# Two gated layers with routed experts: SyncE's DMAs at both joins in other places, a second PSUM bank for four shared experts, and waits in place of the barrier behind the experts

## Chip, core and metric

The program runs on one core of a Trainium2 chip. The metric is the device time of one execution in microseconds (us), given as the median of several executions.

## What is computed

`x` has 64 blocks of 128 tokens with 256 features. Four steps follow each other, each with a gate and a residual:

```python
x = x + tanh(g_xattn[0]) * attention0(layernorm(x), ctx)      # 16 heads, softmax over 128 keys
x = x + tanh(g_ffn[0])   * experts(layernorm(x))              # 64 experts, 8 a token, at most 256 tokens each
x = x + tanh(g_xattn[1]) * attention1(layernorm(x), ctx, mask)
x = x + tanh(g_ffn[1])   * quantised_ffn(layernorm(x))        # needs a maximum over all tokens
# inside experts:
shared = silu(x @ shared_gate.T) * (x @ shared_up.T) @ shared_down.T      # for every token
return routed + shared
```

## The kernel before

**Stages.** The program has one instruction stream per engine, written out by hand, and semaphores between them. Its order: attention 0 with routing (64 blocks, in slots that each hold pieces of up to ten blocks), the experts, attention 1, and two passes of the quantised feed-forward. SyncE (`sp`) issues almost all DMAs, strictly in program order; a wait on it holds up everything behind. `phase_end` (line 270) is a barrier: an engine drains, adds 1 to `phase_done` and waits for a count. Barrier 2 (all five engines) stands between attention 0 and the experts, barrier 3 (TensorE, ScalarE, VectorE) between the experts and attention 1.

**Attention 0** (`attention_sp`, `attention_pe`, ...). In slot s, `stage(lag)` is block s - lag. Per slot SyncE loads a block's context and x, stores the block for the experts to accumulate on (`store`), its normalised tokens transposed (`store_transposed`, into `tokens_t`), its row with gate weights (`store_row`) and its routing counts (`store_steps`, read back by `load_steps`). Some slots near the end carry extra loads: `ffn_weights_in` (the feed-forward's weights, and the first four context pairs, `load_pair`), `first_expert_weights`, `attention_weights(sp, 1, ...)` and `load_shared`.

**Experts** (`expert_slots`). Slot s has, on TensorE: `slot_steps`, `rows_t` (transposes of gathered rows), `keys_or_values`, `up`, `shared_down`, `down`, `shared_up`. Routed expert s, s-1 and s-2 are at different steps of it. GpSimd gathers an expert's 256 rows (2 indirect DMAs) and adds its results (2 more). Two other strands of 64 pieces each are spread over the slots by tables: `PAIR_AT` places the keys and values of attention 1 (`keys_or_values` on TensorE, `copy_pair` on ScalarE, `keep_pair` on SyncE), and `SHARED_AT` the shared expert of 128 tokens (`shared_up`, `shared_tanh`, `shared_silu`, `shared_down`, `shared_out`, `keep_shared`). Slots that a table leaves out have no such piece. The first pieces run in attention 0's last slots and ahead of barrier 2, the last ones behind the last routed expert (slots E+1 to E+4, E = 64).

**Banks.** A shared expert's products stay in one PSUM bank from `shared_up` until `shared_out` has read it. Pieces 0 and 1 have banks 7 and 4, all later ones bank 7, so that

```python
            if n < SHARED_EARLY:
                pe.wait_ge(sem("at_out"), NB)
                pe.wait_ge(sem("qm_done"), NB)
            else:
                wait(pe, "sh_out", n)
```

makes the next `shared_up` wait for ScalarE's `shared_out` of the piece before it. Bank 4 is `down`'s bank from expert 0 on, and attention 1's.

**The second join.** `first_sums` (slot `SUMS_AT` = E + 5 on SyncE) waits for all additions of the experts, then loads for blocks 0 and 1 both halves of the routed sum and the shared part. GpSimd adds the halves (`experts_sum`), VectorE adds the row and makes the statistics (`first_sum`, `first_stats`), GpSimd raises to -1/2, ScalarE normalises (`normalise_first`), TensorE transposes (`transposes`). In attention 1 SyncE's slot loads keys and values (`load_keys_values`) and sums (`load_sums`) of later blocks.

## Time and profile before

| | us |
|---|---|
| median of three runs | 1859.84 (1858.9 to 1864.16) |
| the profiled execution, its own time | 1864.53 |
| its span | 1862.8 |
| TensorE busy / weight loads | 1724.2 / 1349.8 |
| VectorE busy | 1386.4 |
| ScalarE busy | 1180.8 |
| GpSimd busy | 612.5 |

Times in the profile are counted from the span's start. Attention 0 fills the stretch to about 638, the experts that from about 652 to 1137, attention 1 begins at 1156. PE is TensorE, DVE VectorE, ACT ScalarE, POOL GpSimd, SPq SyncE's issuing of DMAs. The granted clock is a share of TensorE's full speed.

### The profile page before, as it was taken

The page shows a single profiled execution, that of the slowest core. Times are in us where ns is not written, and L with a number is a line of the kernel's source. Part 1 is how long each engine was busy: PE and PEld are TensorE (multiplying, and loading weights), DVE is VectorE, ACT ScalarE, POOL GpSimd, SP SyncE. Part 2 cuts the span into 40 slices and gives each one's busy share as a digit, 9 for nine tenths or more (in the row PEclk, how much of TensorE's full clock was granted, in tenths as well). Part 3 has the DMA queues.
Part 4 walks back from the last instruction along what each step waited for, and adds up shares of the span by engine and source line. Part 5 has one row for each costly group of instructions (what it writes and reads, how often), then busy time and mean ns, then how long its engine had stood idle before and what let it go on. Part 6 is the DMA issues. An engine that isn't in the chain of part 4 may idle for free.

```text
span 1862.8 us, 54548 instructions
## 1 busy us (share of the span) xinstructions
PE 1724.2 (93%) x20198; PEld 1349.8 (72%) x20208; DVE 1386.4 (74%) x4589; ACT 1180.8 (63%) x2411; POOL 612.5 (33%) x617
## 2 busy tenths in 40 slices
PE   5999999999999799999999998899999999968855
PEld 4788888888887578888888887677777777733334
DVE  4788888888888637655454544788888888759988
ACT  2777777777777423333333333788888888858875
POOL 1000000000000037777777774222223222211147
PEclk8999999999999999999999999999999999989989
DMA  3233333333324558989898886233323322213265
GB/s 97 69 94 94 97 97 97 103 98 98 94 94 146 171 163 208 233 210 229 214 220 215 219 196 142 87 93 94 89 87 91 97 88 87 59 57 136 102 268 184
DMA packets 231350, 247.65 MB, mean 133 GB/s; under 512 B 29680, under 2 KB 207216, under 8 KB 228912
## 3 DMA queue, kind: packets, MB, share of 16 engines
q1 hardware_dynamic: 206272, 205.54, 34.4%
q0 software_dynamic: 24816, 38.62, 11.5%
q8 instruction: 164, 2.69, 0.6%
q14 instruction: 98, 0.80, 0.2%
HBM read 142.40 MB, written 101.66 MB: 131 GB/s over the span
## 4 chain that ended last, share of the span: by engine, by line
PE 63%; DVE 24%; ACT 8%; issue 2%; DMA 1%; SPq 1%; POOLq 0%; POOL 0%; DVEq 0%; ACTq 0%
DVE mt L928 15%; PE tiles L454 8%; PE tiles L437 8%; PE bank L519 6%; ACT pt L689 6%; PE bank L398 6%; PE tiles L1437 6%; PE bank L382 6%; PE bank L482 3%; PE tiles L421 3%; PE bank L549 3%; PE bank L1449 3%; PE bank L408 3%; DVE hmax L1824 3%; PE tiles L1419 2%
## 5 line engine op out<-in xcount | busy, mean ns | idle before, releaser
L2084 POOL TENSOR_TENSOR rstd<-var,minus_half 128x2 f32<-128x2 f32 x140 | 97.9, 699 | 728.7 <-DVE var L1007 710.0
L928 DVE TENSOR_REDUCE mt<-tiles 128x16 f32<-128x2048 f32 x128 | 293.5, 2293 | 58.8 <-PE tiles L437 58.8
L689 ACT ACTIVATE pt<-tiles 128x2048 f32<-128x2048 f32 x128 | 240.7, 1881 | 48.7 <-PE tiles L454 48.7
L1610 POOL DMA_INDIRECT accumulator<-ye,tid x128 | 208.4, 1628 | 87.6 <-DVE ye L1554 59.0
L1554 DVE TENSOR_SCALAR ye<-bank,xr 128x256 f32<-128x256 f32 x128 | 56.0, 479 | 157.5 <-PE bank L1449 157.5
L1595 POOL DMA_INDIRECT xr<-token_rows,tid x128 | 137.4, 1074 | 78.8 <-DVE tid L1530 41.2
L519 PE MATMUL bank<-xt,w_q 128*128 128x128 f32 x1024 | 156.3, 287 | 0.9 <-ACT xt L697 0.9
L454 PE MATMUL tiles<-qm,qkp 32*128 32x128 f32 x4096 | 151.1, 284 | 6.2 <-DVE mt L928 2.3
L437 PE MATMUL tiles<-qkp 32*128 32x256 f32 x2048 | 150.6, 407 | 3.3 <-ACT qkp L711 3.3
L454 PEld LDWEIGHTS tiles<-qm,qkp 32*128 32x128 f32 x4096 | 126.6, 187 | 35.8 <-DVE mt L928 21.1
L519 PEld LDWEIGHTS bank<-xt,w_q 128*128 128x128 f32 x1024 | 133.1, 196 | 14.7 <-issue 12.9
L482 PE MATMUL bank<-pt,vx 128*32 128x128 f32 x4096 | 139.2, 277 | 2.7 <-ACT pt L689 1.7
L482 PEld LDWEIGHTS bank<-pt,vx 128*32 128x32 f32 x4096 | 104.6, 110 | 45.3 <-issue 40.8
L549 PE MATMUL bank<-w_o,at 128*128 128x256 f32 x512 | 131.8, 380 | 0.5 <-ACT at L778 0.5
L437 PEld LDWEIGHTS tiles<-qkp 32*128 32x128 f32 x2048 | 87.3, 185 | 42.7 <-issue 27.1
L665 ACT ACTIVATE res<-bank 128x256 f32<-128x256 f32 x64 | 24.6, 385 | 143.7 <-PE bank L398 139.3
L940 DVE SCALAR_TENSOR_TENSOR qm<-bank,keep,qkp 128x256 f32<-128x256 f32 x256 | 110.1, 472 | 6.6 <-PE bank L468 6.3
L2107 POOL TENSOR_TENSOR res<-res,bias 128x256 f32<-128x256 f32 x64 | 46.8, 731 | 200.7 <-ACT xn L746 200.7
L709 ACT ACTIVATE qkp<-bank,qb 128x128 f32<-128x128 f32 x256 | 88.8, 372 | 34.3 <-PE bank L519 34.2
L711 ACT ACTIVATE qkp<-bank,kb,keep 128x128 f32<-128x128 f32 x256 | 106.2, 483 | 0.0
L724 ACT ACTIVATE qkp<-cxax,kb,keep 128x128 f32<-128x128 f32 x256 | 105.4, 485 | 0.0
L549 PEld LDWEIGHTS bank<-w_o,at 128*128 128x128 f32 x512 | 87.3, 190 | 8.0 <-ACT at L778 0.7
(252 smaller groups left out, 4098.2 us busy)
## 6 DMA issues: line engine op xcount, KB each, us to landing
keys_values<-res SPq DMA_DIRECT2D x64, 256.0 KB, 3.0
cxax<-keys_values SPq DMA_DIRECT2D x128, 128.0 KB, 2.5
cxax<-accumulator SPq DMA_DIRECT2D x128, 128.0 KB, 2.3
hidden_away<-h_ring SPq DMA_DIRECT2D x8, 1536.0 KB, 5.1
token_rows<-pay SPq DMA_DIRECT2D x64, 160.0 KB, 1.8
pt<-in_expert_up SPq DMA_DIRECT2D x36, 256.0 KB, 3.5
cxax<-in_ctx SPq DMA_DIRECT2D x64, 128.0 KB, 2.2
res<-in_x SPq DMA_DIRECT2D x64, 128.0 KB, 2.3
```

The source lines that it names most:

```text
L382: last = nc.tensor.matmul(kv_bank(n)[:, k * D:(k + 1) * D], weights_, moving, start=(c == 0), stop=(c == KC - 1))
L398: last = nc.tensor.matmul(shared_bank(n)[:, m * FS + j * P:m * FS + (j + 1) * P], w[:, c, j * P:(j + 1) * P], sxt[n % SHARED_IN][:, c, :], ...
L437: last = nc.tensor.matmul(both, qt[r % 2][rows, j, :], kp[r][rows, :, j, :], start=(L == 0), stop=True, skip_group_check=(L == 1))
L454: last = nc.tensor.matmul(tiles[:, i, n * P:(n + 1) * P], kp[r][rows, e, j, :], qm[rows, e, j, :], start=(L == 0), stop=True, skip_group_c ...
L482: last = nc.tensor.matmul(bank[7][32 * h:32 * h + 32, g * P:(g + 1) * P], vx[r][:, GH * g + h, :], pt[p][:, i, n * P:(n + 1) * P], start=T ...
L519: last = nc.tensor.matmul(o_, w[:, c, j * P:(j + 1) * P], (cx[r] if n else xt[p])[:, c, :], start=(c == 0), stop=(c == KC - 1))
L549: last = nc.tensor.matmul(bank[6][:, 0:D], at[r % 2][:, c, :], w_o[:, c, :], start=(L == 1 and c == 0), stop=(c == KC - 1))
L689: nc.scalar.activation(pt[r % 2][:, :, :], tiles[:, :, :], ACT.Exp).then_inc(sem("exp_done"), 1)
L928: nc.vector.tensor_reduce(mt[:, :].rearrange("p (i n c) -> p i n c", i=RT, n=2 * KC)[:, :, :, 0], tiles[:, :, :].rearrange("p i (n k) -> p ...
L1437: last = nc.tensor.matmul(bank[2 + p][:, n * CAP:(n + 1) * CAP], w[k][:, c, :], xrt[p][:, c, :], start=(c == 0), stop=(c == KC - 1))
L1595: nc.gpsimd.indirect_dma_start(out=xr[n % ROWS_IN][:, h, :], out_offset=None, in_=rows[:, :], in_offset=bass.IndirectOffsetOnAxis(ap=tid[n ...
L1610: nc.gpsimd.indirect_dma_start(out=acc[p][:, :], out_offset=bass.IndirectOffsetOnAxis(ap=tid[b % 8][:, h:h + 1], axis=0), in_=ye[r][:, h, ...
```

## The change

- SyncE in attention 0: `ffn_weights_in` comes behind the slot's stores, and no longer loads the first context pairs; these come in the two next slots, also behind the stores. `load_shared` comes a slot earlier. Of the weights of experts 1 to 6, those of 1 to 3 stay in their place, 4 and 5 go behind the last stores and 6 behind `keep_pair`; the last `load_steps` goes ahead of `keep_pair`. Layer 1's `attention_weights` go into expert slot 6 (`ATTENTION_IN_AT`), on the same semaphore as the key and value weights.
- Shared experts 3 and 62 get bank 4 (1 had it); a `shared_up` next to one of these waits only for the output two before it. Expert 0's `down` waits for shared output 3, and shared expert 62 for the last reading of bank 4.
- `PAIR_AT` leaves out 13 slots instead of 11, and its last two pieces run in new slots E+5 and E+6; `keep_pair` of these two is issued in attention 1's slots (`LATE_KEPT`). `SHARED_AT` leaves out slot 57 instead of 54.
- `first_sums` comes in slot E+4.
- Barrier 3 is gone. ScalarE's first normalisation waits for the last `down`, and TensorE's first transpose for all shared outputs and all copies of keys and values.

```diff
-        PHASES = {1: 5, 2: 10, 3: 13, 4: 18, 5: 23}
+        PHASES = {1: 5, 2: 10, 4: 15, 5: 20}
...
-            for s in range(-MAP_AHEAD, E + 6):
+            for s in range(-MAP_AHEAD, E + 7):
...
-        PAIR_AT = numbered([-7, -6, -5, -4, -3, -2, -1] + [s for s in range(E) if s not in (5, 9, 14, 21, 27, 33, 39, 45, 51, 57, 62)]
-                           + [E + 1, E + 2, E + 3, E + 4])
-        SHARED_AT = numbered([-5, -4, -3, -2, -1] + [s for s in range(E) if s not in (8, 20, 23, 30, 36, 42, 48, 54)]
+        SHARED_IN_FOUR = (1, 3, NB - 2)
+        LATE_KEPT = {2: E - 2, 3: E - 1}
+        PAIR_AT = numbered([-7, -6, -5, -4, -3, -2, -1] + [s for s in range(E) if s not in (5, 9, 14, 19, 24, 29, 34, 39, 44, 49, 54, 59, 62)]
+                           + [E + 1, E + 2, E + 3, E + 4, E + 5, E + 6])
+        SHARED_AT = numbered([-5, -4, -3, -2, -1] + [s for s in range(E) if s not in (8, 20, 23, 30, 36, 42, 48, 57)]
...
-            return bank[4] if n < SHARED_EARLY and n % 2 else bank[7]
+            return bank[4] if n in SHARED_IN_FOUR else bank[7]
...
+            elif n in SHARED_IN_FOUR or n - 1 in SHARED_IN_FOUR:
+                pe.wait_ge(sem("sh_out"), n - 1)
             else:
-                wait(pe, "sh_out", n)
+                pe.wait_ge(sem("sh_out"), n)
+            if n == NB - 2:
+                pe.wait_ge(sem("e_y_done"), E)
...
+                    if b == 0:
+                        pe.wait_ge(sem("sh_out"), NB)
+                        pe.wait_ge(sem("kv_out"), E)
...
+                if L == 1 and b == 0:
+                    act.wait_ge(sem("e_down_done"), E)
...
-        FIRST_SUMS, SUMS_AT = 2, E + 5
+        FIRST_SUMS, SUMS_AT = 2, E + 4
...
                         load_sums(sp, stage(-3))
+                        if stage(-3)[0] in LATE_KEPT:
+                            n = LATE_KEPT[stage(-3)[0]]
+                            keep_pair(sp, (n, n))
...
-                    if stage(4) is not None and stage(4)[0] == NB - 1:
-                        sp.wait_ge(sem("o_done_0"), NB)
-                        attention_weights(sp, 1, "w_in")
-                    if stage(5) is not None and stage(5)[0] == NB - 1:
-                        for n in range(SHARED_IN):
-                            load_shared(sp, (n, n))
-                    if stage(5) is not None and stage(5)[0] == ROOM_TO:
-                        ffn_weights_in(sp)
                     load_steps(stage(7))
                     store_steps(stage(6))
                     store(stage(4))
+                    if stage(4) is not None and stage(4)[0] == NB - 1:
+                        for n in range(SHARED_IN):
+                            load_shared(sp, (n, n))
                     store_transposed(stage(5))
+                    if stage(5) is not None and stage(5)[0] == ROOM_TO:
+                        ffn_weights_in(sp)
+                    if stage(5) is not None and ROOM_TO < stage(5)[0] <= ROOM_TO + 2:
+                        for j in range(2):
+                            load_pair(sp, 2 * (stage(5)[0] - ROOM_TO - 1) + j)
...
-                        first_expert_weights(sp, EARLY_FREE, WEIGHT_BUFFERS)
+                        first_expert_weights(sp, EARLY_FREE, 4)
...
             if L == 0:
+                first_expert_weights(sp, 4, 6)
+                load_steps((NB - 1, (NB - 1) % 4))
                 for n in range(KV_EARLY - 1):
                     keep_pair(sp, (n, n))
-                load_steps((NB - 1, (NB - 1) % 4))
+                first_expert_weights(sp, 6, WEIGHT_BUFFERS)
...
-                keep_pair(sp, PAIR_AT.get(s - 1))
+                if s <= E + 5:
+                    keep_pair(sp, PAIR_AT.get(s - 1))
                 keep_shared(sp, SHARED_AT.get(s - 2))
+                if stage(0) is not None and stage(0)[0] == ATTENTION_IN_AT:
+                    attention_weights(sp, 1, "w_in")
...
+                if b == 0:
+                    pe.wait_ge(sem("sh_out"), 4)
```

The other edits drop the three `phase_end(..., 3)`, renumber the waits on `w_in`, and take `load_pair` out of `ffn_weights_in`.

**SyncE, last blocks of attention 0, before.** The names are destination and source; `res` with `tokens_t` is `load_shared`, `table_rows` with `steps_out` is `store_steps`.

```order
L1956 DMA w_o<-in_L_xattn_wo 128x2x256
L1958 DMA bias_col<-in_L_xattn_bq 128x2
L1958 DMA bias_col<-in_L_xattn_bk 128x2
L1958 DMA bias_col<-in_L_xattn_bv 128x2
L1959 DMA bias<-in_L_xattn_bo 128x256
L1298 DMA table<-table_rows 2x4160
L1289 DMA table_rows<-steps_out 64x130
L1266 DMA accumulator<-res 128x256
L1267 DMA accumulator<-zt 128x256
L1274 DMA tokens_t<-x2t 128x256
L1281 DMA token_rows<-pay 128x320
L1200 DMA res<-tokens_t 128x256 x3
```

The same place in the changed kernel (its own line numbers):

```order
L1292 DMA token_rows<-pay 128x320
L1309 DMA table<-table_rows 2x4160
L1300 DMA table_rows<-steps_out 64x130
L1277 DMA accumulator<-res 128x256
L1278 DMA accumulator<-zt 128x256
L1211 DMA res<-tokens_t 128x256 x3
L1285 DMA tokens_t<-x2t 128x256
L1292 DMA token_rows<-pay 128x320
```

The six attention weights are gone from here, and the three loads of tokens stand ahead of the last two stores of this slot.

**SyncE, its last DMAs ahead of barrier 2, before:**

```order
L1298 DMA table<-table_rows 2x4160
L1289 DMA table_rows<-steps_out 64x130
L1281 DMA token_rows<-pay 128x320
L1189 DMA keys_values<-res 128x512 x2
L1662 DMA res<-in_ctx 128x2x128 x2
L1189 DMA keys_values<-res 128x512
L1298 DMA table<-table_rows 2x4160
```

and in the changed kernel:

```order
L1309 DMA table<-table_rows 2x4160
L1300 DMA table_rows<-steps_out 64x130
L1292 DMA token_rows<-pay 128x320
L1370 DMA pt<-in_expert_up 128x512
L1371 DMA on<-in_L_ffn_w 128x256
L1370 DMA qm<-in_expert_up 128x512
L1371 DMA xt<-in_L_ffn_w 128x256
L1309 DMA table<-table_rows 2x4160
L1200 DMA keys_values<-res 128x512 x2
L1681 DMA res<-in_ctx 128x2x128 x2
L1200 DMA keys_values<-res 128x512
L1370 DMA cxax<-in_expert_up 128x512
```

The last reading of the table now has four loads of weights ahead of it, and the stores of keys and values behind it.

**TensorE, end of the experts, before.** `w_k` and `w_v` are pieces of `keys_or_values`, `w_sg` and `w_su` a `shared_up`, `w_sd` a `shared_down`, `ident,xn` attention 1's first transpose.

```order
L382 MATMUL bank<-res,w_k 128x256 x4
L408 MATMUL bank<-w_sd,res 128x256 x2
L398 MATMUL bank<-res,w_sg 128x128 x4
L398 MATMUL bank<-res,w_su 128x128 x4
L382 MATMUL bank<-w_v,res 128x256 x4
L408 MATMUL bank<-w_sd,res 128x256 x2
L499 MATMUL bank<-ident,xn 128x128 x2
```

and in the changed kernel:

```order
L384 MATMUL bank<-res,w_k 128x256 x4
L414 MATMUL bank<-w_sd,res 128x256 x2
L404 MATMUL bank<-res,w_sg 128x128 x4
L404 MATMUL bank<-res,w_su 128x128 x4
L384 MATMUL bank<-w_v,res 128x256 x4
L414 MATMUL bank<-w_sd,res 128x256 x2
L384 MATMUL bank<-res,w_k 128x256 x4
L384 MATMUL bank<-w_v,res 128x256 x4
L508 MATMUL bank<-ident,xn 128x128 x2
```

Two pieces of keys and values now stand behind the last shared expert.

## Rows read from the trace of the kernel before

**Rows 1.** The page, the chain that ended last: share by engine.
```profile
PE 63%; DVE 24%; ACT 8%; issue 2%; DMA 1%; SPq 1%; POOLq 0%; POOL 0%; DVEq 0%; ACTq 0%
```
**Rows 2.** Windows: start:end, length, busy us (xcount) of the engines, clock, DMA share, GB/s.
```profile
750.00:850.00 100.00, 100.00 (x600) 87.55 (x599) 59.85 (x214) 33.97 (x68) 76.09 (x55) 1.00 0.89 224
1050.00:1136.00 86.00, 85.90 (x506) 75.56 (x505) 40.63 (x141) 26.15 (x55) 59.12 (x44) 1.00 0.79 186
1155.00:1160.00 5.00, 3.37 (x28) 2.42 (x28) 3.81 (x10) 3.60 (x10) 3.12 (x5) 0.50 0.40 111
1175.00:1180.00 5.00, 5.00 (x70) 3.47 (x70) 3.40 (x5) 1.37 (x5) 1.19 (x2) 0.63 0.01 3
```
**Rows 3.** Chain in order of time, first join: start us, us, what.
```profile
639.69 2.42 DMA tokens_t<-x2t
...
646.40 2.14 DMA keys_values<-res
649.04 2.71 DMA table<-table_rows
651.88 0.23 PE bank L1392
```
**Rows 4.** Timeline, SyncE's queue, end of attention 0.
```profile
582.95 5.86 SPq L1662 DMA_DIRECT2D res<-in_ctx  x8
...
630.14 0.43 SPq L1354 DMA_DIRECT2D pt<-in_expert_up  x1
...
634.41 0.43 SPq L1956 DMA_DIRECT2D w_q<-in_L_xattn_wq  x1
...
640.76 1.43 SPq L1200 DMA_DIRECT2D res<-tokens_t  x3
```
**Rows 5.** Timeline, VectorE and ScalarE, end of attention 0.
```profile
589.13 2.29 DVE L928 TENSOR_REDUCE mt<-tiles 128x16 f32<-128x2048 f32 x1 [0.39 <-PE tiles L437]
600.04 2.29 DVE L928 TENSOR_REDUCE mt<-tiles 128x16 f32<-128x2048 f32 x1 [1.53 <-PE tiles L437]
...
595.14 0.37 ACT L788 COPY x2t<-bank 128x256 f32<-128x256 f32 x1 [1.71 <-DMA tokens_t<-x2t]
640.95 0.27 ACT L798 CAST steps_out<-bank 64x129 bf16<-64x129 f32 x1 [4.19 <-DMA table_rows<-steps_out]
649.71 0.19 ACT L2122 ACTIVATE sig<-clips 128x2 f32<-128x2 f32 x1
```
**Rows 6.** Timeline, TensorE, first join.
```profile
638.20 0.22 PE L608 MATMUL bank<-fall,sel 128*64 128x129 bf16 x1
643.14 2.07 PE L398 MATMUL bank<-res,w_sg 128*128 128x128 f32 x8 [4.71 <-DMA res<-tokens_t]
652.99 3.68 PE L382 MATMUL bank<-res,w_k 128*128 128x256 f32 x8
658.19 1.13 PE L398 MATMUL bank<-res,w_sg 128*128 128x128 f32 x8 [0.66 <-ACT res L675]
```
**Rows 7.** Timeline, TensorE, second join.
```profile
1136.66 1.05 PE L398 MATMUL bank<-res,w_sg 128*128 128x128 f32 x8
1138.44 1.89 PE L382 MATMUL bank<-w_v,res 128*128 128x256 f32 x8
1140.17 1.03 PE L408 MATMUL bank<-w_sd,res 128*128 128x256 f32 x4
1156.17 0.66 PE L499 MATMUL bank<-ident,xn 128*128 128x128 f32 x2 [4.43 <-ACT xn L746]
```
**Rows 8.** Timelines of ScalarE and GpSimd, second join.
```profile
1150.92 0.59 ACT L657 COPY res<-bank 128x512 f32<-128x512 f32 x1 [1.34 <-PE bank L382]
1155.47 0.60 ACT L746 ACTIVATE xn<-res,nmr,rstd 128x256 f32<-128x256 f32 x1 [3.22 <-DVE nmr L1011]
1141.14 1.56 POOL L1610 DMA_INDIRECT accumulator<-ye,tid x1 [0.30 <-issue]
```

**Rows 9.** Chain in order of time, second join.
```profile
1148.37 3.28 DMA res<-shared_out
```

More of the change, by code:

```diff
@@ L370, in keys_or_values @@
             if n == 0:
-                pe.wait_ge(sem("wkv_in"), 16 * 2)
+                pe.wait_ge(sem("w_in"), 16 * 10)
                 pe.wait_ge(sem("exp_done"), NB)
@@ L1562, in next_layer @@
                 elif e[0] == E // 4 + 4:
-                    dve.wait_ge(sem("w_in"), 16 * 14)
+                    dve.wait_ge(sem("w_in"), 16 * 16)
                     scale_queries(dve, 1)
@@ L1650, in ffn_weights_in @@
             sp.dma_start(wdraw[:, :, :], a["L1_ffn_w_down"].rearrange("(k p) i -> p k i", p=P)).then_inc(sem("ffn_w_in2"), 16)
-            for j in range(4):
-                load_pair(sp, j)
         def ffn_weights_out(sp, n):
@@ L1702, in flamingo_gated_two_layers @@
         MASKS_IN_AT = {2: 0, 4: 1}
+        ATTENTION_IN_AT = 6
         def ffn_chunks(body, nb, more):
@@ L1962, in keys_values_weights @@
             for dst, src in ((w_k, "L1_xattn_wk"), (w_v, "L1_xattn_wv")):
-                sp.dma_start(dst[:, :, :], a[src].rearrange("(k p) n -> p k n", p=P)).then_inc(sem("wkv_in"), 16)
+                sp.dma_start(dst[:, :, :], a[src].rearrange("(k p) n -> p k n", p=P)).then_inc(sem("w_in"), 16)
         def scale_queries(dve, L):
@@ L2124, in _ @@
             experts_act(act)
-            phase_end(act, 3)
             attention_act(act, 1)
@@ L2142, in _ @@
             experts_pe(pe)
-            phase_end(pe, 3)
             attention_pe(pe, 1)
@@ L2196, in _ @@
             experts_dve(dve)
-            phase_end(dve, 3)
             attention_dve(dve, 1)
```

## Prediction

> **What bounds the kernel now.** I read the chain that ended last, then the windows, then the timelines of each engine at the two joins. The chain lies 63% on TensorE and 24% on VectorE [rows 1]. In the experts TensorE alone bounds: it is busy 100.00 of 100 us and 85.90 of 86 at the stage's end, at full clock [rows 2]. So a piece of TensorE work that leaves this stage shortens it by its whole length, and a delay of the stage's start moves everything behind it. The edits lie where this does not hold, at the joins.
>
> At the first join the chain leaves the compute engines: a store of tokens, loads of them, stores of keys and values, the last load of the table, barrier, TensorE [rows 3]. SyncE's queue makes it late. From 626 to 634 it issues weights of six experts, from 634.41 six loads for attention 1, and only at 640.76 the three loads of tokens [rows 4]. TensorE ends routing at 638.42 and waits 4.71 us for them [rows 6]. ScalarE's last piece ahead of the barrier ends at 649.90 [rows 5], but SyncE holds the barrier until the table of 649.04 has landed, 2.71 us later; TensorE goes on at 651.88 [rows 3].
>
> At the second join the sums are requested from 1147.5 on, the last load of a block takes 3.28 us to land [rows 9], and GpSimd, VectorE and ScalarE follow before TensorE's first transpose at 1156.17, after 4.43 us of idle time [rows 7].
>
> **The change, part by part.** Everything is counted in the profiled execution, whose own time is 1864.53.
>
> *Feed-forward weights behind the stores.* SyncE's burst has eight context loads alone for 5.86 us [rows 4], with five loads of weights ahead of them and the slot's stores behind. ScalarE then waits 1.71 us for a store of tokens, and VectorE's maxima are 10.91 us apart (589.13 to 600.04) [rows 5]; one slot takes 9.15 us by its neighbours, 10.91 less the 1.76 that this stall makes of it. With the stores first and the contexts in two later slots the stall goes: **1.8 us**. Bounds: 0, where the landing and not the issue is late, and 1.8.
>
> *First join.* The third of the early experts' weights starts at 630.14 and its pair of issues ends at 631.05. An issue takes 0.48 us (three in 1.43) [rows 4]. Five others (row, table, counts, block, zeros) bring SyncE to 633.6, where it now issues the tokens; landing as before (640.76 to 643.14, 2.4 us) they are there at 636, ahead of TensorE's 638.42. So the shared experts start 4.7 us earlier, and their strand, 6.8 us long (643.14 to 649.90) [rows 5, 6], ends at 645.2 or, at full clock, 644.2. ScalarE's wait of 4.19 us for a store of counts [rows 5] goes too, since ten issues ahead of that store are gone. SyncE: the last counts are on it at 638.9; store, row (0.6) and four weights (1.9) end at 641.7; the table's load needs 2.7 to land, 644.4. Behind it stand two stores of keys and values, two contexts, a third store that waits 2.1 us for the first one [rows 3], and two weights: SyncE ends at 645.9. The barrier opens there, TensorE starts at 646.1 instead of 651.88: **5.8 us**. Bounds: 7.2, where only the other engines' 644.2 to 645.2 count and I have put two issues too many, and 3, if the landings in this crowded stretch take twice as long. I take the middle way since each step is a row.
>
> *Two banks.* Behind the barrier TensorE waits 0.66 us ahead of each `shared_up` for ScalarE's `shared_out` [rows 6], five times until expert 0's `down` fills the gap. Pieces 2, 3 and 4 lose the wait, 5 and 6 keep it, as bank 4 is taken: 3 x 0.66 = **2.0 us**. Hidden below it is only ScalarE and VectorE's part of a piece, covered by the 1.7 us of keys and values. Bounds 0.7 and 2.0.
>
> *Two pairs fewer in the experts.* A piece of keys and values is 1.73 us of TensorE (1138.44 to 1140.17) [rows 7]. Two leave: **3.5 us**, all of it while TensorE bounds. GpSimd is the cover: it is busy 76.09 us of 100 with 55 pieces [rows 2], and about 0.3 us stands between them [rows 8], so 92 of 100. The stage is 485 us for 68 slots (651.88 to 1136.66), 7.1 each, and GpSimd needs 0.92 of that, 6.5; 3.5 us less leave it room. Bounds 0 and 3.5.
>
> *Second join.* Measured from the last routed expert (1136.66), TensorE has 15.1 us of work and waits (1156.17 less 4.43 is 1151.74) [rows 7]. It gains two pieces (+3.5), loses two waits of 0.66 (-1.3), and the last piece waits for ScalarE's copy of the one before, in the same bank (+0.8, from the 0.59 of a copy) [rows 8]: 18.1. ScalarE must copy it (0.59) and normalise (0.60) [rows 8], so the first transpose comes at 19.4; it came at 19.5. The sums are ready earlier: GpSimd's last addition starts at 1141.14 [rows 8] and lands some 4 us later, 8.5 after the mark, where the loads came at 10.8; their chain of 8.7 us ends at 17.2. So the sums stop being late and TensorE's own strand, with ScalarE behind, is what comes last: **0.1 us**, bounds -1 and 2. The barrier itself is free either way: its three engines are done at about 1152, with TensorE's strand, and the data are not.
>
> *Waits added.* ScalarE's for the last `down` and TensorE's for all outputs hold nothing, since both engines come there later by program order. SyncE's store of pair 62 now stands ahead of block 3's sums and waits for a copy 16 us behind the mark; block 3 is needed some 8 us later. Six loads more in slot 6 cost SyncE 3 us of a 7.1 us slot in which it has half free. Nothing.
>
> *Clock.* TensorE's granted clock fell after idle stretches: eight products of keys and values took 3.68 us behind the first barrier [rows 6] against 1.89 at full clock [rows 7], and the granted clock was 0.50 in 1155 to 1160 [rows 2], the lower of its two levels, behind the idle 4.43. At the second join idle time shrinks to some 1.3 us in one piece. Full clock would give back half of 3.37 us of busy time, 1.7; I take **1.0** for both joins, with 0 and 5.3 as ends (1.7, 1.8 behind the barrier, and 0.37 x 5.0 in 1175 to 1180 [rows 2]).
>
> The Trainium skill ("TensorE: Matmul & The Clock Gate", "What's actually happening") says that the throttled level is the default and activity releases it. By that rule both joins, emptier before, would run warmer now, and the sum would be some 3 us more; the trace agrees as far as the fall behind idle goes, but it also shows a fall at 1175 with TensorE at work.
>
> Sum: 1.8 + 5.8 + 2.0 + 3.5 + 0.1 + 1.0 = 14.2. The profiled execution would take 1850.3. The median of the runs shown is 4.7 lower than that execution, so I forecast **1845.6 us**.
>
> **Rivals.**
> 1. *The clock stays up at both joins.* For: less idle time at both. Against: some 3 us of idle time are left ahead of the first barrier (643 to 646), and the fall at 1175. It gives 5.3 where I took 1.0: 1841.3. Chance 0.13.
> 2. *GpSimd becomes the bound of the experts.* Slots without a pair take TensorE some 5.4 us (7.1 less 1.7), an expert takes GpSimd 6.5, and there are 13 instead of 11 of them. Then the 3.5 us come back as waits for rows: 1849.1. Against: TensorE never waited with 11. Chance 0.12.
> 3. *The DMA engines, not SyncE's order, made the stores and tokens late.* Then the first term goes and half of the second: 1845.6 + 1.8 + 2.9 = 1850.3. Against: TensorE's wait of 4.71 ends 2.4 us after the issue, a usual landing. Chance 0.08. The Trainium skill ("DMA: Bandwidth & Descriptors", "Rules for kernel authors") holds that all issuing engines feed the same 16 DMA engines; if their backlog decides, another place in the queue buys nothing, which is this rival.
> 4. *The order was covered anyway*, and what is won at the joins is waited for later (attention 1 at the same time as before): about 1860. Chance 0.03.
> 5. *Slower: gathered rows come late.* DMA engines are at 0.89 in the experts [rows 2]. Denser TensorE work and six more loads could push the gathers beyond their lead, so that TensorE waits for each expert's rows. It decides from (14.2 + 5.6) / 64 = 0.31 us per expert; at 0.5 it gives 1845.6 + 32 = 1878. Against: not one wait for rows now. Chance 0.02.
>
> **The numbers.** My forecast has the rest, 0.62, and alone reaches from 1842 to 1850. The range takes in rivals 1 and most of 2 and 3: 1839 to 1852. A measurement can tell 0.3%, 5.6 us, from no change, so faster means below 1854.3: cases 1 to 3 and the forecast make 0.95, less 0.02 for several terms at their low ends: 0.93. Within 0.3%: 0.05. Slower: 0.02.
>
> **What would show it.** Maxima of VectorE 9.15 apart throughout the last full slots; TensorE's first shared expert right behind the last counts, without a wait for tokens; its first piece behind the barrier 7 to 8 us earlier than 651.88; no wait ahead of the shared experts 2 to 4; last routed expert 13 us earlier than 1136.66; first transpose 19 to 20 us behind it, and released by ScalarE's copy, not by the sums. Wrong would be a wait of TensorE in the experts, a barrier still held past 648 by a landing, or a first transpose over 21 us behind the last expert.

## The result, and the profile after

| | before | changed |
|---|---|---|
| median, us | 1860.47 (1856.15 to 1864.74, 12 executions) | 1850.94 (1843.01 to 1855.44, 12 executions) |
| ratio to before | | 0.9949, 95% interval 0.9936 to 0.9962 |
| the profiled execution: own time / span | 1864.53 / 1862.8 | 1851.82 / 1850.1 |

The change makes the kernel 9.5 us faster in the medians; 14.2 were forecast. The profiled executions differ by 12.7, but not all of that is the change's: VectorE's maximum at 570.82 before stands at 568.32 after, in a stretch that nothing of the change touches. So spans can't be compared to the microsecond here, and I compare stretches between marks that both traces have. The mark "last `down`" is the first product behind it (1136.66 before, 1123.33 after), as in the prediction.

| stretch, us | before | after | gain | forecast |
|---|---|---|---|---|
| start to the maximum at 570.82 / 568.32 | 570.82 | 568.32 | 2.50 | not the change's |
| from there to the last counts (PE `fall,sel`) | 67.38 | 65.60 | 1.78 | 1.8 |
| last counts to TensorE's first piece behind the barrier | 13.68 | 9.89 | 3.79 | 5.8 |
| from there to expert 0's `down` | 38.54 | 36.74 | 1.80 | 2.0 |
| expert 0's `down` to the last `down` | 446.24 | 442.79 | 3.45 | 3.5 |
| last `down` to the first transpose of attention 1 | 19.51 | 19.06 | 0.45 | 0.1 |
| first transpose to ScalarE's second exponential | 24.86 | 26.09 | -1.23 | 1.0, clock, both joins |
| second exponential to the end | 681.8 | 681.6 | 0.2 | 0 |

The stretches that the change touches give 10.0 (1.78 + 3.79 + 1.80 + 3.45 + 0.45 - 1.23), near the 9.5 of the medians.

One execution of all the runs below, of e7_fill_first, took 1993.12 us at a mean granted clock of 0.84 and is left out of the medians and ratios.

The page of after, share of the chain by engine, against [rows 1]: the shape of the kernel is the same.

```profile
PE 64%; DVE 24%; ACT 8%; issue 2%; SPq 1%; DMA 1%; POOLq 0%; POOL 0%; DVEq 0%; ACTq 0%
```

Windows of after: the experts ([rows 2] before), then the first join and the ramp of attention 1.

```profile
640.00:645.00 5.00, 0.51 (x3) 0.23 (x3) 0.48 (x2) 0.00 (x0) 0.00 (x0) 0.82 0.89 292
645.00:650.00 5.00, 5.00 (x13) 3.98 (x13) 1.27 (x8) 0.58 (x1) 2.18 (x2) 0.50 0.74 226
750.00:850.00 100.00, 100.00 (x607) 87.78 (x607) 59.45 (x217) 33.33 (x67) 75.77 (x56) 1.00 0.89 220
...
1147.00:1152.00 5.00, 4.06 (x26) 2.88 (x23) 3.76 (x5) 2.80 (x9) 1.30 (x2) 0.50 0.46 133
1152.00:1157.00 5.00, 5.00 (x42) 3.54 (x43) 3.38 (x6) 2.00 (x5) 2.12 (x3) 0.50 0.43 131
```

TensorE still fills the experts entirely (100.00 of 100), with GpSimd at 75.77, so two pieces fewer count in full. But directly behind the first barrier, and for ten microseconds of the ramp (the first slots of attention 1, until its engines follow each other without gaps), the granted clock is 0.50, the lower of its two levels.

**End of attention 0.** Timelines of VectorE and ScalarE, against [rows 5]:

```profile
586.61 2.29 DVE L939 TENSOR_REDUCE mt<-tiles 128x16 f32<-128x2048 f32 x1 [0.38 <-PE tiles L443]
595.76 2.29 DVE L939 TENSOR_REDUCE mt<-tiles 128x16 f32<-128x2048 f32 x1 [0.45 <-PE tiles L443]
...
590.87 0.37 ACT L799 COPY x2t<-bank 128x256 f32<-128x256 f32 x1
```

The maxima are 9.15 apart where one gap was 10.91, and ScalarE's copy no longer waits for a store of tokens.

**First join.** SyncE's queue of after; the mark is the last counts at 633.92:

```profile
634.56 0.48 SPq L1309 DMA_DIRECT2D table<-table_rows  x1
635.09 0.48 SPq L1300 DMA_DIRECT2D table_rows<-steps_out  x1
635.61 0.58 SPq L1292 DMA_DIRECT2D token_rows<-pay  x1
636.23 0.43 SPq L1370 DMA_DIRECT2D pt<-in_expert_up  x1
...
638.21 0.48 SPq L1309 DMA_DIRECT2D table<-table_rows  x1
638.74 0.87 SPq L1200 DMA_DIRECT2D keys_values<-res  x2
639.66 1.25 SPq L1681 DMA_DIRECT2D res<-in_ctx  x2
642.06 0.34 SPq L1200 DMA_DIRECT2D keys_values<-res  x1
642.44 0.44 SPq L1370 DMA_DIRECT2D cxax<-in_expert_up  x1
642.92 0.45 SPq L1371 DMA_DIRECT2D xt<-in_L_ffn_w  x1
```

The chain of after over the same stretch, in order of time, against [rows 3]:

```profile
632.41 2.14 DMA table_rows<-steps_out
...
638.74 3.25 DMA keys_values<-res
...
642.06 0.34 SPq L1200
```

The third store of keys and values waits for the first one to land, 3.25 us after that one's issue (2.14 before [rows 3]); for 1.1 of them SyncE is idle, and the weights of expert 6 stand behind it. SyncE reaches the barrier at 643.4. TensorE, against [rows 6]:

```profile
633.92 0.22 PE L617 MATMUL bank<-fall,sel 128*64 128x129 bf16 x1
...
643.81 0.22 PE L1411 MATMUL bank<-table,halves_tri 128*128 128x32 bf16 x1 [5.04 <-SPq L272]
644.71 0.40 PE L1423 MATMUL bank<-table,begun 64*128 64x130 bf16 x2 [0.68 <-DVE begun L1532]
645.03 3.78 PE L384 MATMUL bank<-res,w_k 128*128 128x256 f32 x8
648.61 1.75 PE L414 MATMUL bank<-w_sd,res 128*128 128x256 f32 x4
650.19 1.05 PE L404 MATMUL bank<-res,w_sg 128*128 128x128 f32 x8
...
665.77 1.13 PE L404 MATMUL bank<-res,w_sg 128*128 128x128 f32 x8 [0.66 <-ACT res L684]
```

The wait of 4.71 us for tokens is gone, and 5.04 us of waiting for SyncE at the barrier has come in its place. The first eight products of keys and values behind it take 3.78 us, as they took 3.68 before. The wait of 0.66 us for ScalarE is left only from the fifth piece on.

**Second join.** TensorE of after, against [rows 7], and ScalarE, against [rows 8]:

```profile
1139.26 1.97 PE L384 MATMUL bank<-w_v,res 128*128 128x256 f32 x8 [0.77 <-ACT res L666]
1142.40 0.44 PE L508 MATMUL bank<-ident,xn 128*128 128x128 f32 x2 [1.17 <-ACT xn L757]
```

```profile
1141.26 0.58 ACT L666 COPY res<-bank 128x512 f32<-128x512 f32 x1 [2.15 <-PE bank L384]
1141.74 0.60 ACT L757 ACTIVATE xn<-res,nmr,rstd 128x256 f32<-128x256 f32 x1
```

The first transpose comes behind ScalarE's normalisation, which comes behind its copy of the last piece. The sums are no longer late: VectorE has the statistics' last value at 1138.28 + 0.69, 2.8 us before ScalarE uses it:

```profile
1138.28 0.69 DVE L1022 SCALAR_TENSOR_TENSOR nmr<-mv,rstd 128x2 f32<-128x2 f32 x1 [0.83 <-POOL rstd L2104]
```

### The profile page after: what moved, and what is told of

Its sections match the earlier page's. It is cut to its first block, busy times and chain, and to the rows that moved or that the text cites. A ratio compares the mean times of both kernels' runs of the same rounds, so it can differ in the third digit from the quotient of the medians.

```text
span 1850.1 us, 54546 instructions
## 1 busy us (share of the span) xinstructions
PE 1720.9 (93%) x20198; PEld 1348.2 (73%) x20208; DVE 1385.3 (75%) x4589; ACT 1179.3 (64%) x2411; POOL 611.1 (33%) x617
## 4 chain that ended last, share of the span: by engine, by line
PE 64%; DVE 24%; ACT 8%; issue 2%; SPq 1%; DMA 1%; POOLq 0%; POOL 0%; DVEq 0%; ACTq 0%
DVE mt L939 15%; PE tiles L460 8%; PE tiles L443 8%; PE bank L528 7%; ACT pt L698 6%; PE bank L404 6%; PE tiles L1456 6%; PE bank L384 6%; PE bank L488 4%; PE bank L558 3%; PE tiles L427 3%; PE bank L1470 3%; PE bank L414 3%; DVE hmax L1844 3%; PE tiles L1438 2%; DVE h_ring L1837 2%
```

## The experiments

Twelve kernels ran, in three groups (e1 to e4, e5 to e8, e9 to e12), each group on one chip with the kernel before beside it (medians 1858.78, 1860.08 and 1858.84). All are the changed kernel with one edit, or with several edits that add to each other. The stretches are those of the table above:

| run | counts to barrier | to first `down` | to last `down` | to transpose | to 2nd exp. | median | ratio to before |
|---|---|---|---|---|---|---|---|
| changed kernel | 9.89 | 36.74 | 442.79 | 19.06 | 26.09 | 1850.94 | 0.9949 [0.9936, 0.9962] |
| e1_burst_back | 9.65 | 35.96 | 442.78 | 19.07 | 24.28 | 1850.19 | 0.995 [0.993, 0.9969] |
| e2_one_bank | 9.81 | 39.59 | 442.79 | 20.81 | 24.28 | 1853.12 | 0.9955 [0.9936, 0.9974] |
| e3_eleven_out | 10.48 | 35.62 | 446.24 | 17.27 | 25.64 | 1851.6 | 0.9963 [0.995, 0.9977] |
| e4_late_six | 7.69 | 36.98 | 442.79 | 19.06 | 25.34 | 1846.73 | 0.9937 [0.9915, 0.996] |
| e5_barrier3 | 9.19 | 36.23 | 442.79 | 22.19 | 25.09 | 1853.25 | 0.9973 [0.996, 0.9985] |
| e6_sums_late | 9.47 | 37.24 | 442.79 | 19.06 | 23.80 | 1851.26 | 0.9958 [0.9941, 0.9975] |
| e7_fill_first | 11.04 | 34.16 | 442.79 | 19.07 | 24.22 | 1851.83 | 0.9959 [0.9936, 0.9982] |
| e8_fill_second | 10.08 | 36.98 | 442.79 | 19.00 | 23.64 | 1849.77 | 0.9934 [0.9909, 0.9959] |
| e9_join1 | 6.04 | 34.98 | 442.79 | 19.06 | 24.27 | 1844.63 | 0.9925 [0.9907, 0.9943] |
| e10_join1_banks | 5.93 | 32.58 | 443.02 | 17.91 | 24.23 | 1841.35 | 0.9905 [0.989, 0.9921] |
| e11_join1_banks_fill | 6.14 | 33.57 | 442.79 | 17.92 | 22.03 | 1839.83 | 0.9899 [0.9882, 0.9916] |
| e12_again | 9.54 | 36.08 | 442.78 | 19.07 | 24.28 | 1848.03 | 0.9939 [0.9923, 0.9955] |

The medians of one kernel, the changed one, are 1850.94 and 1848.03 in two groups, so only differences of several microseconds show in them; the stretches carry the readings. Each stretch is from one profiled execution of its kernel. How far they move by chance can be seen where the edits touch nothing: among the kernels that have the changed kernel's work ahead of the barrier the first stretch is 9.19 to 10.48, and among those that have its work on both sides of TensorE's wait there the second is 35.62 to 37.24.

### Taking the parts back

**e1_burst_back.** The feed-forward's weights and four pairs of contexts go ahead of the slot's stores again:

```diff
+                    if stage(5) is not None and stage(5)[0] == ROOM_TO:
+                        ffn_weights_in(sp)
+                        for j in range(4):
+                            load_pair(sp, j)
                     load_steps(stage(7))
                     store_steps(stage(6))
```

> The changed kernel, but the feed-forward weights and the first four context pairs are again issued in one burst ahead of the slot's stores. Theory (the stall of 1.7 us came from the place in SyncE's queue): one gap between VectorE's maxima near 590 us is 10.9 us again instead of 9.15, and the last counts come 1.8 us later against the start of that stretch; total +1.8 us. Rival (the DMA engines were late, the place does not matter): all gaps stay 9.15, total 0.

One gap between VectorE's maxima is 10.33 again (586.90 to 597.23) where it is 9.15 without the edit, and ScalarE waits for the store of tokens:

```profile
592.33 0.37 ACT L799 COPY x2t<-bank 128x256 f32<-128x256 f32 x1 [1.13 <-DMA tokens_t<-x2t]
```

So the mechanism is right, and the rival (all gaps stay 9.15) falls; the stall is 1.18 here and was 1.76 before. The rest of the way to the counts was a further 1.25 longer, from a low clock behind 620 which e12_again, without this edit, shows too (granted clock 0.67 in 620 to 625). The second join is as in the changed kernel, 19.07.

**e2_one_bank.** Only piece 1 has bank 4, as before, and each `shared_up` waits for the output before it:

```diff
-        SHARED_IN_FOUR = (1, 3, NB - 2)
+        SHARED_IN_FOUR = (1,)
...
-            elif n in SHARED_IN_FOUR or n - 1 in SHARED_IN_FOUR:
-                pe.wait_ge(sem("sh_out"), n - 1)
```

> The changed kernel, but shared experts 3 and 62 are back in bank 7 and every shared_up from piece 2 on waits for the output just before it. Theory (the bank is what TensorE waits for): waits of 0.66 us come back ahead of pieces 2, 3, 4 and behind the experts ahead of 62 and 63; first piece behind barrier 2 to shared_up of piece 5 takes 23.8 us instead of 22.0, last expert to first transpose 20.4 instead of 19.1; total +3.1 us. Rival (ScalarE's and VectorE's part of a piece sets the pace): both stretches stay as they are, total 0.

Three waits come back behind the barrier, where the stretch is 2.85 us longer, two come back at the second join, where it is 1.75 longer (3.1 in all were expected for both). One wait is printed as 0.66, but costs 0.9: the pieces behind the barrier stand 5.68 apart with it, 4.79 without it (TensorE's `w_sg` products of this kernel, then of after):

```profile
651.79 1.13 PE L402 MATMUL bank<-res,w_sg 128*128 128x128 f32 x8 [0.66 <-ACT res L682]
657.47 1.13 PE L402 MATMUL bank<-res,w_sg 128*128 128x128 f32 x8 [0.66 <-ACT res L682]
```

```profile
654.98 1.05 PE L404 MATMUL bank<-res,w_sg 128*128 128x128 f32 x8
...
659.77 1.05 PE L404 MATMUL bank<-res,w_sg 128*128 128x128 f32 x8
```

The products themselves take 1.13 instead of 1.05 behind a wait, and their first weight load starts only 0.03 us ahead of the first product, where it starts 0.21 ahead without the wait (657.44 and 654.77).

**e3_eleven_out.** `PAIR_AT` leaves out eleven slots as before, its last pieces are not late, and `SHARED_AT` leaves out 54.

> The changed kernel, but the table of keys and values leaves out the 11 slots of before again and has no pieces in slots E+5 and E+6 (shared table with 54, as before). Theory (TensorE bounds the experts, a piece is worth its 1.73 us there, and behind them the sums' chain is what comes last, so leaving the two pieces there shortens nothing): experts 3.5 us longer; last expert to first transpose 17 to 17.5 us instead of 19.1, by the chain of the sums from their earlier place; total +1.5 to 2.0 us. Rival A (the sums still need what they needed, 19.5): total +3.9 us. Rival B (GpSimd bounds): experts the same length, total -1.7 us.

The experts take 446.24 again, the second join 1.8 less. So two pairs out of the experts gain 3.45 there and cost 1.79 at the join: 1.66 net. The second join is not bound by TensorE here: it idles 3.98 us ahead of the first transpose, and ScalarE's normalisation follows VectorE's last statistic, which ends at 1142.95. So the chain of the sums takes 17.27, where the prediction put it at 17.2.

```profile
1143.63 0.69 PE L508 MATMUL bank<-ident,xn 128*128 128x128 f32 x2 [3.98 <-ACT xn L757]
```

**e5_barrier3.** Barrier 3 is back on TensorE, ScalarE and VectorE.

> The changed kernel with barrier 3 put back between the experts and attention 1. Theory (the barrier hid behind the sums before; now that TensorE's own strand comes last, its drain and the wait for each other stand on the path): last expert to first transpose 19.1 + 0.2 to 1.5 us, the first sum of VectorE later than before the last copy; total +0.2 to 1.5 us. Rival (barrier free): 19.1, total 0. Rival (its removal was a main gain): over 3 us more.

It costs 3.1 us (22.19 instead of 19.06), more than the 0.2 to 1.5 that I gave it, and as much as the second rival had. VectorE's first sum now waits for the barrier:

```profile
1136.63 0.42 DVE L981 TENSOR_TENSOR res<-res,cxax 128x256 f32<-128x256 f32 x1 [6.48 <-ACTq L272]
```

It starts 18.6 us behind the last `down` (12.8 without barrier), so the 3.6 us of statistics and normalisation, which ran beside TensorE's last pieces, now come behind them. Before the change the sums themselves came later (requested from 1147.5 on), so the barrier could be free there; no run takes it out of that kernel alone.

**e6_sums_late.** `first_sums` goes back to slot E+5.

> The changed kernel with the first sums asked for one expert slot later again (E+5). Theory (they are ready some 2 us ahead of ScalarE, so half of the shift is slack): the issue comes at about 10.6 us behind the last expert (behind a store that waits for ScalarE) instead of 8.7, first transpose 19.1 to 19.5 us behind it; total 0 to +0.5 us. Rival (the sums are still last): +1.9 us.

19.06 as without the edit: the last statistic comes 1.0 us later against the last `down` and still ahead of ScalarE, so the slack of the sums covers a slot, and undoing this part alone costs nothing.

### What holds the first barrier

**e4_late_six.** The third `keep_pair` and the weights of expert 6 come behind the barrier:

```diff
-                for n in range(KV_EARLY - 1):
+                for n in range(KV_EARLY - 2):
                     keep_pair(sp, (n, n))
-                first_expert_weights(sp, 6, WEIGHT_BUFFERS)
...
             phase_end(sp, 2)
+            keep_pair(sp, (KV_EARLY - 2, KV_EARLY - 2))
+            first_expert_weights(sp, 6, WEIGHT_BUFFERS)
```

> The changed kernel, but the third store of keys and values and the two weights of expert 6 are issued right behind barrier 2 instead of ahead of it. Theory (SyncE's wait for the first store and what stands behind it hold the barrier, the step that my prediction priced too low): the barrier opens when the table has landed, near 641.0 in the changed kernel's time, so last counts to first piece behind the barrier takes 7.1 us instead of 9.9; total -2.8 us. Rival (the landing of the table is itself late, at about 643, or another engine is last): 9.9 stays, total 0.

2.2 us come back at the join and none is lost later; 2.8 were expected. TensorE starts at 637.41, 0.43 behind SyncE's last issue ahead of the barrier (635.70 + 1.28), and SyncE shows no wait for the table there:

```profile
634.25 0.48 SPq L1309 DMA_DIRECT2D table<-table_rows  x1
634.78 0.88 SPq L1200 DMA_DIRECT2D keys_values<-res  x2
635.70 1.28 SPq L1680 DMA_DIRECT2D res<-in_ctx  x2
638.27 0.34 SPq L1200 DMA_DIRECT2D keys_values<-res  x1
```

**e9_join1.** Beyond that, the table is loaded directly behind the last stores, and the weights of experts 4 and 5 come behind the barrier too.

> The changed kernel, but at the first join only the stores of the first pairs, the table of steps right behind them, keep_pair 0 and keep_pair 1 stand ahead of the barrier; keep_pair 2 and the weights of experts 4, 5 and 6 are issued behind it. Theory (what stands ahead of the barrier on SyncE's queue sets its time; the third keep_pair waited 3.3 us for the first store to land, and each context or weight issued ahead costs its issue): from the last counts to the first piece behind the barrier about 6.3 us instead of 9.9 (late_six alone gave 7.7), so 3.5 us less, with the experts' own stretch (442.8) and the second join (19.1) as they were; median near 1847. Rival A (GpSimd or the table's own landing holds the barrier at about 7.5 us): gain 2.4 at most, median 1848.5. Rival B (the weights of 4 to 6 then come late, and a wait behind loads shows among the first seven experts): stretch from the first down to the last above 444, median 1850 or more.

6.04 us where 6.3 was expected, and 1844.63 beside 1848.03 of the unedited kernel in the same group; neither rival came. TensorE waits 1.19 us at the barrier, and its next eight products run at full clock:

```profile
641.18 0.22 PE L1409 MATMUL bank<-table,halves_tri 128*128 128x32 bf16 x1 [1.19 <-SPq L272]
642.07 0.28 PE L1421 MATMUL bank<-table,begun 64*128 64x130 bf16 x2 [0.67 <-DVE begun L1530]
642.29 1.99 PE L384 MATMUL bank<-res,w_k 128*128 128x256 f32 x8
```

Against e12_again that is 3.5 us at the barrier, and 1.8 for these products, of which a wait of 0.56 for VectorE two pieces later takes back a part (1.1 is left).

The chain of this kernel shows two landings on SyncE's queue:

```profile
635.88 2.41 DMA table_rows<-steps_out
...
638.83 2.44 DMA keys_values<-res
```

The last load of the table now waits for the store of counts to land, which is what is left ahead of the barrier besides the issues. And the first store of keys and values lands after 2.44 us with no weights issued ahead of it; in the nine other kernels whose chain shows this landing, all with four loads of weights ahead of it, it took 3.19 to 4.46.

**e10_join1_banks.** In addition, shared piece 5 gets bank 1, and pair 62 bank 0:

```diff
-            return bank[n % 4] if n < KV_EARLY else bank[5]
+            return bank[n % 4] if n < KV_EARLY else bank[0] if n == E - 2 else bank[5]
...
-            return bank[4] if n in SHARED_IN_FOUR else bank[7]
+            return bank[4] if n in SHARED_IN_FOUR else bank[1] if n == 5 else bank[7]
```

(pair 62 then waits for bank 0's last reading, and pair 63 and the shared pieces 5 and 6 for the copy two before.)

> The same, and two banks in turn also for the pieces 5 and 6 behind the barrier and for the pairs 62 and 63 in the ramp. Theory (each wait of TensorE for ScalarE's copy out of the one bank costs 0.9 us, as one_bank showed): the barrier to the first down shorter by 1.8 us (36.7 to about 35), the last down to the first transpose by 0.9 (19.1 to about 18.1); median near 1844.5. Rival (VectorE or ScalarE, not TensorE, ends last in the ramp, so that the wait ahead of pair 63 hid beside them): the second difference is 0, median 1845.3.

The two waits behind the barrier are gone, 2.40 us with the 0.56 of e9_join1 among them, and the second join is 1.15 shorter (1.8 and 0.9 were expected; the rival's 0 for the second falls). All six executions (1839.49 to 1842.45) lie below all six of e12_again (1845.41 to 1849.67). This version beats both kernels, 6.7 us below the changed one and 17.5 below the one before.

### The clock

**e7_fill_first.** TensorE runs 40 small products, whose results nobody reads, ahead of the first barrier.

> The changed kernel with 40 products of 128x256 in bf16 (about 4.3 us at full clock) put on TensorE behind its last piece ahead of barrier 2, where it idles 5.0 us; their results are overwritten unread. Theory (the idle time ahead of the barrier drops the clock, which is why the first slot behind it is slow): the eight products of keys and values behind the barrier take 1.9 to 2.0 us instead of 3.78 and the shared_down 1.03 instead of 1.75; first piece to piece 5's shared_up 22.0 becomes 19.4; total -2.6 us. Rival (they are slow for another reason, such as DMAs landing in the same memory): durations stay, total 0.

The clock stays at full level and the products behind the barrier take 1.99 instead of 3.78; the stretch behind the barrier is 2.6 us shorter. But in this execution the barrier opened 1.15 us later: the first store of keys and values took 4.46 us to land (3.25 in after), and the third store waited for it on SyncE. The two context loads between them took 2.50 us to issue (1.25 in after), but were done at 640.86, 1.0 ahead of that landing. Whether the fill has a part in it is open; e3_eleven_out has a landing of 4.29 without fill. The median shows no gain. The chain first, then SyncE's and TensorE's timelines:

```profile
637.44 4.46 DMA keys_values<-res
...
638.36 2.50 SPq L1681 DMA_DIRECT2D res<-in_ctx  x2
...
644.82 1.99 PE L384 MATMUL bank<-res,w_k 128*128 128x256 f32 x8
```

**e8_fill_second.** 28 unread products stand in the gaps of the second join and of the ramp.

> The changed kernel with short runs of bf16 products (128x512, some 0.22 us each, 28 in all) at TensorE's waits in the second join and in attention 1's first three slots, each run shorter than its wait; results overwritten unread. Theory (idle time in the ramp drops the clock twice, and the slow stretches are what the second join gave back): granted clock 1.00 from the last expert on, first transpose to second exponential 20.5 to 22 us instead of 26.1; total -4 to -5 us. Rival (the ramp is bound by VectorE and ScalarE, the clock is slack): clock 1.00 and the stretch stays at 24 to 26 us. Second rival: the fill does not hold the clock.

23.64 where 20.5 to 22 was expected, just below what kernels without them show (23.80 to 26.09): the granted clock is 1.00 until 1152, but 0.92 in 1152 to 1157 and 0.73 in 1157 to 1162. So this fill did not hold the clock, as the second rival had it. I concluded that the ramp hung on VectorE and ScalarE, which was too early.

**e11_join1_banks_fill.** The same unread products, three fewer, on top of e10_join1_banks.

> The same, with 25 unread products of TensorE in the gaps of the ramp, whose results nobody reads. Theory (the low clock in the ramp costs at most what ScalarE and VectorE don't cover; fill_second got 23.6 where unfilled kernels had 23.8 to 26.1): transpose to second exponential 23.6 to 24.0, the rest as in the kernel without them; median lower by 0 to 1.5 us, near 1844. Rival (the clock is what bounds the ramp): 21 to 22, median near 1842.

Here the clock never fell (1.00 from 1130 to 1165), and the stretch took 22.03, beside 24.23 without them. My expectation (23.6 to 24.0) fell, the rival's 21 to 22 is right. Windows of e10_join1_banks, then of this kernel, whose ramp begins at 1133.7 and 1135.4:

```profile
1135.00:1140.00 5.00, 4.41 (x43) 2.55 (x41) 2.76 (x6) 4.79 (x13) 3.07 (x6) 0.53 0.38 123
1140.00:1145.00 5.00, 4.01 (x43) 2.98 (x43) 4.72 (x8) 2.73 (x8) 1.93 (x3) 0.78 0.35 108
...
1150.00:1155.00 5.00, 3.97 (x67) 2.91 (x68) 2.66 (x4) 3.52 (x7) 0.91 (x2) 0.74 0.24 61
```

```profile
1135.00:1140.00 5.00, 4.64 (x51) 2.61 (x49) 2.18 (x6) 4.47 (x13) 3.62 (x6) 1.00 0.43 138
1140.00:1145.00 5.00, 4.74 (x55) 2.99 (x52) 4.81 (x9) 4.05 (x12) 2.15 (x4) 1.00 0.66 195
...
1150.00:1155.00 5.00, 5.00 (x80) 3.12 (x79) 2.49 (x4) 3.86 (x7) 1.24 (x2) 1.00 0.18 54
```

So the low clock of the ramp costs 2.2 us in this pair, 1.8 to 4.1 against the unfilled kernels' 23.80 to 26.09. In the medians 1.5 are left (1841.35 to 1839.83) and the ranges of the two overlap; whether the fill pays over many executions stays open.

**e12_again.** The changed kernel unedited.

> The changed kernel itself once more, on the same chip and in the same rounds as the three above, so that they can be compared with it directly. Both theories: the stretches of the first profile within half a microsecond where no low clock moves (9.9, 36.7, 442.8, 19.1), the ramp anywhere from 23.8 to 26.1, and the ratio to the kernel before 0.995 with an interval that overlaps 0.9936 to 0.9962.

As expected but for the clock: 9.54, 442.78 and 19.07 as in the first trace, 36.08 against 36.74, and 24.28 where the first profile had 26.09. The 36.08 is the clock too: the first `shared_down` behind the barrier takes 1.09 us, not 1.75.

## Why the prediction was right, and where it was not

The direction and the range held (1850.94 within 1839 to 1852), the size did not: 14.2 forecast, 9.5 measured. The forecast's own median for before was 0.6 low; the rest is in the first-join term and in the clock.

- **Feed-forward weights behind the stores, 1.8: right.** 1.78 measured between marks, 1.18 of it coming back as a stall when undone. The mark-to-mark stretch is 65.6 us in ten of the twelve traces that keep this part, and 67.0 in e3_eleven_out and e12_again, so a single execution could have hidden most of it.
- **First join, 5.8: mis-sized, 3.8.** The wait for tokens and ScalarE's for the store of counts are gone as forecast. The step that failed is "a third store that waits 2.1 us for the first one": 2.14 came from a trace where no weights were in flight beside it, and with four loads of weights and the table issued just ahead of it the landing takes 3.25. e9_join1, without the weights but with the table, has 2.44, and the kernels with weights 3.19 to 4.46. Two more pieces of it: the table is issued 4.3 us behind the counts and not 3.5, because a load of the table, itself behind a landing (632.41 + 2.14), stands ahead of the last store of counts, and because store, row and weights take 3.1 (635.09 to 638.21) where the sum put 2.8; its own terms give about 3.0. And TensorE starts 0.4 behind SyncE, not 0.2. That makes 1.1 + 0.8 + 0.2, about the missing 2.0. Chance adds little here: with the same queue the stretch is 9.2 to 10.5 us (11.0 with fill), a gain of 2.6 to 4.5, and 5.8 in none. I had kept as bounds 3 and 7.2, and the lower one rested on just this landing. e4_late_six and e9_join1 show that what stands ahead of the barrier on SyncE counts: 2.2 us, and 3.5 in all, come back when it goes behind it.
- **Two banks, 2.0: 1.8, near by luck.** Each wait is worth 0.9 and not 0.66, 2.7 for three. But how long the clock stays low behind the barrier differs from execution to execution, and the first piece carries it. From the barrier's opening to the first `w_sg` products it was 6.31 us before, with the wait (651.88 [rows 3] to 658.19 [rows 6]), and is 6.38 in after without it (643.81 to 650.19); in the seven other kernels with the same work there, without wait or fill, it is 5.26 to 6.51. Where the clock is up it is 3.80 (e9_join1, e7_fill_first). So in this pair the first of the three waits went without gain and 1.8 are left; against e12_again, the same program, 2.5 are. e2_one_bank, with wait and low clock, has 7.37 (644.42 to 651.79).
- **Two pairs fewer, 3.5: right**, 3.45, and GpSimd did not become the bound.
- **Second join, 0.1: 0.45.** The first transpose comes 19.06 behind the last `down` and is released by ScalarE behind the last copy, as forecast (19.4). What failed is a sentence beside it, "The barrier itself is free either way": with the sums early it costs 3.1 us (e5_barrier3). That late sums hid it in the kernel before is argued from the order of events there, not shown by a run.
- **Clock, 1.0: wrong sign in this pair of profiles.** Less idle time was to give some of the low clock back. It did not: before, the stretch to the first `w_sg` was 5.4 us without its wait (6.31 less 0.9), and of the eight traces with the change's work there seven have more, 5.60 to 6.51. The shortest, 5.26, stands behind the longest idle time, 5.63 (e3_eleven_out), the longest, 6.51, behind the shortest of these eight, 2.84 (e4_late_six). So the runs show that the clock falls there, not that its length follows the idle time ahead. At the second join it fell in the ramp, where gaps of 0.5 to 1.2 us between TensorE's pieces are left. Over the unfilled kernels the same stretch takes 23.8 to 26.1 us whatever the edit, so -1.2 is mostly the luck of two executions and the honest term was 0. The prediction's "fall at 1175 with TensorE at work" is misread, too: in before the clock was already down in a microsecond in which TensorE did nothing (busy 0.00, clock 0.50), behind one at 0.94; 1175 to 1180 is the end of that low stretch.

```profile
1172.00:1173.00 1.00, 0.00 (x0) 0.00 (x0) 0.38 (x2) 1.00 (x2) 0.29 (x1) 0.50 0.36 107
```

The rivals: GpSimd as bound, gains covered by later waits and late gathered rows all fell, as the experts took 442.79 with TensorE without a gap. Rival 3, that DMA engines and not the order of the queue decide, fell in its main claim: other places in the queue moved the barrier by 3.8, 2.2 and 3.5 us. But a part of it is what shortened my gain: a landing grew from 2.14 to 3.25 us behind weights, and is 2.44 without them (e9_join1). Rival 1 did not come, but what it rests on is real: with the clock up 2.6 us are had behind the first barrier (e7_fill_first) and 2.2 in the ramp (e11_join1_banks_fill). The change by itself doesn't keep it up.

On this last point the Trainium skill ("TensorE: Matmul & The Clock Gate", "What's actually happening") says that the throttled level is the default, that activity releases it, and that how much runs cold varies between executions. The traces agree as far as they reach: eight products take 3.78 us behind 5.04 us of idle time and 1.99 behind 1.19, the clock is full with unread products in the gaps (e11_join1_banks_fill, though not e8_fill_second), and the ramp takes 26.09 against 24.28 in two executions of one program.

## What to carry to other kernels

Where one queue opens a barrier last, as SyncE did here, its issues and landings ahead of it delay the next stage, so put there only what that stage's first instruction needs, and let loads for later stand behind it. A landing taken from a quiet stretch is too short a price where weights are in flight: take the longest one that the trace shows in a crowded stretch. Judge an edit by stretches between marks that both traces share, profile the same kernel more than once before giving a difference of 1 us a cause, and before calling a barrier or a wait free, ask whether that is so only because of the very delay that the edit takes away.

## What was not expected of the hardware

- A wait that the timeline prints as 0.66 us costs 0.9: the products behind it take 1.13 instead of 1.05, and the pieces stand 5.68 apart instead of 4.79.
- The same pair of context loads took SyncE 0.99, 1.25 and 2.50 us to issue in e9_join1, after and e7_fill_first. The store issued just ahead of them landed after 2.44, 3.25 and 4.46 us in the same three; in the last two that landing, not the issue, held the barrier.
- Behind 2.84 us of idle time at the barrier (e4_late_six) eight products took 3.78 us, behind 1.82 (e7_fill_first) and 1.19 (e9_join1) they took 1.99: here an idle stretch of hardly 3 us cost 1.8 more behind it. The length of the low stretch did not follow the idle time: 2.84 us of it were followed by a longer one than 5.63 were (e3_eleven_out, 3.34 us for the eight products).
